# Rows of the destination nodes read from the node table instead of from a second copy by partition, in a four-layer graph network on one core

## The chip, the cores and the metric

One of the cores of a Trainium2 chip runs the whole program; the other cores are idle. The metric is the time of one execution on the device in microseconds, taken several times, with the median given. Beside it stands one execution taken by the hardware profiler, which gives the trace.

## The reference

A network of four graph layers over 50,000 nodes with 64 features and 50,000 edges. The edges are sorted by destination. Before each layer the node features are normalised (layer norm), and what the layer gives is added to them. In short:

```python
h = layernorm(x)
# layer 0: gated convolution, messages summed at dst
z = concat([h[dst], h[src], edge_attr]);  m = sigmoid(z @ W_f + b_f) * softplus(z @ W_s + b_s)
m = m * exp(-distance ** 2 / 9 / 2);      out = segment_sum(m, dst) + h
# layer 1: plain edge network
m = relu(concat([h[src], h[dst], e]) @ W1 + b1) @ W2 + b2;  out = segment_sum(m, dst)
# layer 2: two attention layers of 5 heads (softmax over the edges of a node and a self loop), then a matrix
e = leaky_relu(xl[src] + xr[dst]);        a = softmax over dst of (e . att)
# layer 3: normalised graph convolution W h, batch norm, relu
```

What matters here is that layers 0, 1 and both attention layers need, for each edge, the row `h[src]` (anywhere in the table) and the row `h[dst]`. Since `dst` is sorted, the destinations of 128 neighbouring edges lie close together: some 128 of the 50,000 rows.

## The kernel before, in words

Edges are worked on in 392 tiles (`TILES`) of 128 edges, four tiles to a block (`BLK`), 98 blocks (`NB`) to an edge stage. The program is a sequence of stages; each has its own instruction streams for the five engines and ends when all of them and the DMAs they wait for are done.

1. `setup` (L215 to L552) loads weights and indices and makes lists from them: `lo_i`, for each tile the number of the 128-row block of nodes in which its first destination lies; `rel_d`, for each edge its destination less 128 times that block number; and the list of the tiles whose destinations reach beyond two such blocks.
2. `node_pass(layer)` (L555 to L722) normalises the nodes in 28 groups of 14 tiles of rows (`GRP`), 448 KB each. VectorE writes `h` of a group (L621), in layers 1 and 2 with sums made on ScalarE (L677), in layer 0 with an addition on GpSimd (L656). SyncE then issues, per group, in layer 2 a store of `x` to `x_d` (L715), then `h_d<-h` (L717, the node table, one row of 256 bytes per node), then `near_d<-h` (L718, in layers 0, 1 and 2). `near_d` is a second copy of the table in which row b of partition p is node 128 b + p, so that a partition's own rows lie beside each other and are written in pieces of 3,584 bytes. The ring of `h` buffers comes free when both stores have landed.
3. The edge stages: e0 is `gated_edges` (L931), e1 is `plain_edges` (L1128), l0 and l1 are the two runs of `attention_logits` (L1516). All four use `NearRows` (L791 to L911). GpSimd gathers `h[src]` by an indirect DMA for each tile (`gather`, L870). The rows `h[dst]` are not gathered. `NearRows.load` makes SyncE load, for each tile, the 256 rows of the two blocks that begin at `lo_i[t]` from `near_d` (L882, 64 KB, 512 bytes for each partition), and `relb`, the tile's destinations as offsets, broadcast to all partitions (L877). VectorE compares `relb` with `iota_p`, the number of the row that a partition holds, which gives a one-hot matrix `hotT` (L894). TensorE multiplies it with the rows loaded, onto the transposed `h[src]` (`turn`, L905 and L909). So the destination rows cost a load of neighbouring rows and a matrix product.
4. The far tiles. An edge whose destination lies beyond the window gets its row by a gather: in front of the first block, `fetch_rest`, `mask_rest` and `store_rest` (L823 to L862) run turns of four tiles each (`RING`). In a turn VectorE copies the tile's indices (L838) and a mask (L839), GpSimd gathers the rows of the table (L830), VectorE multiplies them by the mask (L845), and SyncE stores them to `rest_d` (L858); the turn ends when the four stores have landed. `NearRows.load` adds them in again for every block as `z<-rest_d` (L884). `turns` (L813) reads the number of turns from `extra_n`: at least one, else the number of far tiles over four, rounded up. For these inputs 12 tiles reach beyond their two blocks, so each of the four stages runs three turns. The same list tells `extra_pass` (L1392) which sums span more than two blocks.
5. SyncE's order in an edge stage is, for each block, `relb`, a read of four numbers of `lo_i` into registers, the four near loads, `z<-rest_d`, the edge attributes (L976, e0), and the store of the messages of an earlier block (L987, e0). SyncE runs them in that order. Loads are issued up to four blocks (`RINGS`) ahead of TensorE, held back by `z_used`.
6. In l0 and l1 ScalarE's queue loads the destinations of the softmax scan beside that (`acc<-dst_d`, L1486, 15 loads of 200 KB). After l1 the layer goes on as softmax, messages and `attention_nodes` (L1989). With g = 0 the latter writes the table of the second attention layer, `g_d` (L2036), and the copy `near_d<-gout` (L2037, 128 KB, 98 times).

The line that the change touches in every block of every edge stage is L882:

```python
for t in range(BLK):
    sp.dma_start(self.near[k][:, t, :, :], self.S["near_d"][:, ds(los[t], WIN), :]).then_inc(self.near_in[k], 16)
```

Of the kernel before, what the change touches and what calls it, by code (L numbers as in the profile page):

```python
# [21 lines left out]
F32 = mybir.dt.float32  # L22
# [7 lines left out]
P = 128  # L30
# [94 lines left out]
def build(nc, io, out):  # L125
    top = ExitStack()
    with top:
# [6 lines left out]
        h_d = dram("h_d", (TILES * P, C))  # L134
        g_d = dram("g_d", (TILES * P, C))
# [5 lines left out]
        near_d = dram("near_d", (P, TILES + 1, C))  # L141
# [14 lines left out]
        extra_i = sb("extra_i", [1, 3, EXTRA], I32)  # L156
# [58 lines left out]
def setup(nc, io, S):  # L215
# [4 lines left out]
    lo_i, extra_i, extra_n, extra_lo, eps, dst_d = (S[k] for k in ("lo_i", "extra_i", "extra_n", "extra_lo", "eps", "dst_d"))  # L220
    with Phase(nc) as ctx:
# [11 lines left out]
        lo, hi, more, upto, base = (sb(n, [1, TILES]) for n in ("lo", "hi", "more", "upto", "base"))  # L233
        diff_i = sb("diff_i", [1, TILES], I32)
        total_i = sb("total_i", [1, 1], I32)
        col = sb("col", [CT, 2, 4])
        wide_diff = sb("wide_diff", [CT, 4, P])
        step = sb("step", [P, EXTRA])
        passed = sb("passed", [CT, 4, EXTRA])
        a_of = sb("a_of", [P, EXTRA])  # L240
# [5 lines left out]
        turned_col = ctx.enter_context(nc.psum_tensor("turned_col", [P, 2, 4], F32))  # L246
# [90 lines left out]
        with nc.Block() as block:  # L337
            @block.sync
            def _(sp):
# [21 lines left out]
                sp.dma_start(S["near_d"][:, TILES:TILES + 1, :], blank[:, :, 0:C]).then_inc(s_clean, 16)  # L361
# [4 lines left out]
                sp.wait_ge(s_clean, 32)  # L366
# [9 lines left out]
            def _(pool):  # L376
# [7 lines left out]
                nc.gpsimd.iota(S["iota_p"][:, :], pattern=[[P, WIN]], base=0, channel_multiplier=1,  # L384
# [7 lines left out]
            def _(dve):  # L392
# [49 lines left out]
                chain(nc.vector.tensor_tensor_scan(upto[:, :], hi[:, :], more[:, :], 0.0, ALU.mult, ALU.add))  # L442

# [20 lines left out]
                chain(nc.vector.tensor_scalar(a_of[:, :], counted[:, 0, :], float(TILES - 1), None, ALU.min))  # L464
                chain(nc.vector.tensor_copy(extra_i[:, 0, :], a_of[0:1, :]))
                chain(nc.vector.tensor_copy(extra_i[:, 2, 0:1], a_of[0:1, 0:1]))
# [4 lines left out]
                chain(nc.vector.tensor_tensor(extra_i[:, 2, 1:], again[:, 1:], a_of[0:1, 1:], ALU.add))  # L471
# [8 lines left out]
                                                     op0=ALU.mult, op1=ALU.add))  # L480
                dve.sem_inc(s_rel, 1)
# [39 lines left out]
            def _(pe):  # L521
# [12 lines left out]
                nc.tensor.matmul(lo_all[:, :], ones[0:1, :], lo[:, :], start=True, stop=True)  # L534
                pe.wait_ge(s_need, 3)
                for c in range(4):
                    for n, row in enumerate((upto, hi)):
                        mm = nc.tensor.matmul(turned_col[0:CT, n, c:c + 1], row[0:1, c * CT:(c + 1) * CT], ones[0:1, 0:1], start=True, stop=True)
# [3 lines left out]
                pe.wait_ge(s_need, 4)  # L542
# [12 lines left out]
def node_pass(nc, S, layer):  # L555
# [6 lines left out]
    with Phase(nc) as ctx:  # L562
# [23 lines left out]
        def tiles(g):  # L586
            return slice(g * GRP, (g + 1) * GRP)
# [1837 lines left out]
```

## Time and profile before

| what | value |
|---|---|
| median of 3 runs | 6153.05 us (6148.98 to 6160.13) |
| the profiled execution | span 6214.2 us |
| mean granted TensorE clock | 0.845 of full speed |
| busy, of the span: PE, DVE, ACT, POOL | 71%, 53%, 50%, 53% |
| DMA packets, MB | 1,393,493, 665.08 |
| near loads (`near_e`, `near_l`) | 784 + 784 of 64 KB |
| copies `near_d<-h` | 84 of 448 KB |
| copies `near_d<-gout` | 98 of 128 KB |

No time of the profiled execution is listed apart from its span. The span runs from its first instruction to its last and is 61 us, or 1.0%, above the median of the plain runs. The stages lie one behind the other, so a time saved in one of them is saved in the whole, as long as the stage's own limit lies there. The five engines take turns in being the limit: the shares of the whole span say little, and what counts is read stage by stage.

### The profile page before, as it was taken

The page shows a single profiled execution, that of the slowest core. Times are in us where ns is not written, and L with a number is a line of the kernel's source. Part 1 is how long each engine was busy: PE and PEld are TensorE (multiplying, and loading weights), DVE is VectorE, ACT ScalarE, POOL GpSimd, SP SyncE. Part 2 cuts the span into 40 slices and gives each one's busy share as a digit, 9 for nine tenths or more (in the row PEclk, how much of TensorE's full clock was granted, in tenths as well). Part 3 has the DMA queues.
Part 4 walks back from the last instruction along what each step waited for, and adds up shares of the span by engine and source line. Part 5 has one row for each costly group of instructions (what it writes and reads, how often), then busy time and mean ns, then how long its engine had stood idle before and what let it go on. Part 6 is the DMA issues. An engine that isn't in the chain of part 4 may idle for free. (4 is left out here: it accounts for less than half of the span.)

```text
span 6214.2 us, 127051 instructions
## 1 busy us (share of the span) xinstructions
PE 4419.2 (71%) x31655; PEld 3124.8 (50%) x31655; DVE 3312.8 (53%) x7235; ACT 3117.1 (50%) x8158; POOL 3300.7 (53%) x3372
## 2 busy tenths in 40 slices
PE   0078898089896089997498749999669896055564
PEld 0056676066664056665376326666447663054452
DVE  3833333766666432233787963333488788611156
ACT  0267776644555434444386214444358524644447
POOL 0855553155552165553586975555268687666620
PEclk6589998599998599999699979999879998576775
DMA  7545554655554744444133644444323333622224
GB/s 187 169 118 122 123 123 98 176 106 106 109 110 106 241 105 112 113 113 101 33 83 76 153 124 109 113 112 114 83 48 83 77 88 84 138 45 45 44 58 130
DMA packets 1393493, 665.08 MB, mean 107 GB/s; under 512 B 835537, under 2 KB 1341325, under 8 KB 1391594
## 3 DMA queue, kind: packets, MB, share of 16 engines
q1 hardware_dynamic: 1307980, 580.76, 37.4%
q0 software_dynamic: 64256, 65.93, 5.9%
q10 hardware_dynamic: 21124, 17.02, 0.9%
q8 instruction: 35, 0.57, 0.0%
q14 instruction: 98, 0.80, 0.0%
HBM read 393.69 MB, written 269.08 MB: 107 GB/s over the span
## 5 line engine op out<-in xcount | busy, mean ns | idle before, releaser
L870 POOL DMA_INDIRECT z_e<-h_d,src_i x784 | 756.8, 965 | 652.8 <-PE zTp_e L909 453.0
L1656 ACT ACTIVATE leak_l<-tp_l,bcat 128x512 f32<-128x512 f32 x588 | 365.9, 686 | 665.1 <-issue 422.4
L1681 DVE COPY zT_l<-zTp_l 128x512 f32<-128x512 f32 x196 | 135.5, 691 | 1005.7 <-DMA near_d<-gout_a 341.3
L754 ACT ACTIVATE hot_e<-iota_n,rel 128x256 f32<-128x256 f32 x1176 | 501.0, 502 | 322.9 <-DMA hn_a<-g_d 247.2
L784 DVE TENSOR_TENSOR acc<-acc,part_e 128x128 f32 x1176 | 336.8, 286 | 610.1 <-DMA hn_a<-g_d 247.4
L767 PE MATMUL part_e<-z_e,hot_e 128*128 128x128 f32 x1568 | 313.4, 376 | 436.7 <-DVE acc L784 226.9
L870 POOL DMA_INDIRECT z_l<-h_d,src_i x392 | 389.6, 994 | 326.4 <-PE zTp_l L909 229.2
L870 POOL DMA_INDIRECT z_l<-g_d,src_i x392 | 387.9, 989 | 324.9 <-PE zTp_l L909 230.0
L767 PEld LDWEIGHTS part_e<-z_e,hot_e 128*128 128x128 f32 x1568 | 285.2, 279 | 465.0 <-DVE acc L784 240.4
L905 PE MATMUL zTp_e<-ident,z_e 128*128 128x128 f32 x784 | 175.8, 306 | 480.4 <-DMA z_e<-rest_d 472.8
L1351 POOL DMA_INDIRECT z_e<-h_d,src_i x392 | 370.8, 946 | 222.7 <-issue 104.8
L767 PE MATMUL part_e<-m_e,hot_e 128*128 128x128 f32 x3136 | 408.5, 286 | 61.2 <-issue 28.1
L1661 ACT ACTIVATE leak_l<-tp_l,bcat 128x256 f32<-128x256 f32 x784 | 307.8, 475 | 283.1 <-PE tp_l L1618 252.2
L767 PEld LDWEIGHTS part_e<-m_e,hot_e 128*128 128x128 f32 x3136 | 392.5, 200 | 78.4 <-issue 39.9
L767 PEld LDWEIGHTS part_m<-m_m,hot_m 128*128 128x128 f32 x3136 | 365.9, 192 | 88.0 <-DVE acc L784 80.2
L767 PE MATMUL part_m<-m_m,hot_m 128*128 128x128 f32 x3136 | 403.2, 282 | 2.4 <-DVE acc L784 1.1
L1611 PE MATMUL tp_l<-zT_l,wcat 128*128 128x256 f32 x1176 | 376.2, 402 | 22.6 <-DVE zT_l L1681 14.1
L754 ACT ACTIVATE hot_m<-iota_n,rel 128x256 f32<-128x256 f32 x784 | 334.3, 497 | 110.0 <-PE part_m L767 108.5
L905 PEld LDWEIGHTS zTp_e<-ident,z_e 128*128 128x128 f32 x784 | 80.4, 143 | 566.5 <-issue 554.6
L905 PE MATMUL zTp_l<-ident,z_l 128*128 128x128 f32 x784 | 174.1, 304 | 264.8 <-DMA z_l<-rest_d 244.8
L1611 PE MATMUL tp_l<-zT_l,wswap_l 128*128 128x256 f32 x1176 | 355.6, 384 | 1.2 <-issue 1.2
L2179 DVE TENSOR_TENSOR prod_a<-xl_a,wself_a 128x640 f32<-128x640 f32 x392 | 303.9, 815 | 41.7 <-PE xl_a L2073 37.3
(362 smaller groups left out, 11787.7 us busy)
## 6 DMA issues: line engine op xcount, KB each, us to landing
near_e<-near_d SPq DMA_DIRECT2D x784, 64.0 KB
near_l<-near_d SPq DMA_DIRECT2D x784, 64.0 KB
h_d<-h SPq DMA_DIRECT2D x84, 448.0 KB
near_d<-h SPq DMA_DIRECT2D x84, 448.0 KB
m_d<-m_m SPq DMA_DIRECT2D x196, 138.0 KB
relb_e<-rel_d SPq DMA_DIRECT2D x196, 128.0 KB
z_e<-rest_d SPq DMA_DIRECT2D x196, 128.0 KB
relb_l<-rel_d SPq DMA_DIRECT2D x196, 128.0 KB
```

What stands on the lines that cost most here:

```text
L754: ins = self.nc.scalar.activation(self.hots[k][:, t, :], self.S["iota_n"][:, :], ACT.Abs, scale=-1.0, bias=self.S["rel"][:, ds(n * BLK + t ...
L767: mm = self.nc.tensor.matmul(self.parts[t // 2][:, t % 2, w, :], self.hots[k][:, t, w * P:(w + 1) * P], m[:, t, :], start=True, stop=True)
L784: ins = self.nc.vector.tensor_tensor(x, x, part[:, t % 2, :, 0:x.shape[2]], ALU.add)
L870: self.nc.gpsimd.indirect_dma_start(out=self.z[n % RINGS][:, t, SIDES[t % 2]], out_offset=None, in_=self.table[:, :], in_offset=bass.Indir ...
L905: self.nc.tensor.matmul(zTp[:, t * P:(t + 1) * P], self.z[k][:, t, :], ident[:, :], start=(t == 0), stop=False, is_transpose=True, skip_gr ...
L1351: nc.gpsimd.indirect_dma_start(out=z[k][:, t, 0:C], out_offset=None, in_=S["h_d"][:, :], in_offset=bass.IndirectOffsetOnAxis(ap=S["src_i"] ...
L1611: mm = nc.tensor.matmul(by_side(tp[q])[:, side], left[:, q, :], by_side(zT[k])[:, side], start=True, stop=True)
L1656: nc.scalar.activation(leak[u % 2][:, q, :], tp[q][:, :], ACT.Relu, bias=bcat[:, 0, q:q + 1], scale=1.0 - SLOPE).then_inc(leak_ready, 1)
L1661: nc.scalar.activation(by_side(leak[u % 2][:, 3 + q, :])[:, side], tp[3 + side][:, q * 2 * P:(q + 1) * 2 * P].rearrange("p (r e) -> p r e" ...
L1681: nc.vector.tensor_copy(zT[k][:, :], zTp[k][:, :]).then_inc(zT_ready, 1)
L2179: nc.vector.tensor_tensor(prod[k][:, 2 * q:2 * q + 2, :].rearrange("p t (h c) -> p t h c", h=H), xl[slot(u, q)][:, :, 0:HC].rearrange("p t ...
```

## The change

The copy `near_d` is dropped, with all that writes it. The near rows of a tile are loaded from the table itself (`h_d`, or `g_d` in l1), from the tile's first destination on: 256 rows in one piece of 64 KB, of which partition p gets rows 2p and 2p + 1 behind the first. `first_i` holds the first destination of each tile; `ahead` and with it `rel_d` hold each destination less the first one of its tile, and `iota_p` numbers the rows in the new order. Each table gets one more tile of rows, cleared in setup, since a window can reach past the last node. The far tiles of the edge stages get a list of their own, `far_i` with its number of turns in `extra_n[1]`: tiles whose last destination lies 256 or more behind their first. `extra_pass` keeps the old list, and the sums at the destination keep `lo_i` and `rel`. Some buffers move: `digit`, `lof` and `hif` of `plain_edges` into the tail of `acc`, and `din` of `finish` onto `deg_out`.

```diff
-        h_d = dram("h_d", (TILES * P, C))
-        g_d = dram("g_d", (TILES * P, C))
+        h_d = dram("h_d", ((TILES + 1) * P, C))
+        g_d = dram("g_d", ((TILES + 1) * P, C))
-        near_d = dram("near_d", (P, TILES + 1, C))
...
-                sp.dma_start(S["near_d"][:, TILES:TILES + 1, :], blank[:, :, 0:C]).then_inc(s_clean, 16)
+                for table in ("h_d", "g_d"):
+                    sp.dma_start(S[table][TILES * P:(TILES + 1) * P, :].rearrange("(p a) c -> p a c", a=1), blank[:, :, 0:C]).then_inc(s_clean, 16)
...
-                nc.gpsimd.iota(S["iota_p"][:, :], pattern=[[P, WIN]], base=0, channel_multiplier=1,
+                nc.gpsimd.iota(S["iota_p"][:, :], pattern=[[1, WIN]], base=0, channel_multiplier=WIN,
...
+                chain(nc.vector.tensor_copy(first_i[:, :], clipped[0:1, :]))
+                chain(nc.vector.tensor_tensor(wide_one[:, :], ends[:, :], clipped[0:1, :], ALU.subtract))
+                chain(nc.vector.tensor_scalar(wide_one[:, :], wide_one[:, :], float(WIN * P), None, ALU.is_ge))
+                chain(nc.vector.tensor_tensor_scan(far_upto[:, :], hi[:, :], wide_one[:, :], 0.0, ALU.mult, ALU.add))
...
+                chain(nc.vector.tensor_scalar(more[:, 0:1], far_upto[:, TILES - 1:TILES], float(RING - 1), float(RING), ALU.add, ALU.max))
+                chain(nc.vector.tensor_copy(total_i[:, :], more[:, 0:1]))
+                chain(nc.vector.tensor_single_scalar(extra_n[:, 1:2], total_i[:, :], RING.bit_length() - 1, ALU.logical_shift_right))
...
+                    chain(nc.vector.tensor_scalar(far_passed[:, c, :], step[0:CT, :], col[:, 2, c:c + 1], None, ALU.is_ge))
...
+                chain(nc.vector.tensor_tensor(ahead[:, :], dstf[:, :], turned[0][:, :], ALU.subtract))
...
-        outs = 32
+        outs = 32 if layer == 3 else 16
...
-                        sp.dma_start(near_d[:, tiles(g), :], h[k][:, :, :]).then_inc(n_out[two], 16)
...
-        n = eng.value_load(self.S["extra_n"][0:1, 0:1], min_val=1, max_val=EXTRA // RING)
+        n = eng.value_load(self.S["extra_n"][0:1, 1:2], min_val=1, max_val=EXTRA // RING)
...
-        los = self.nc.values_load_multi_w_load_instructions(self.S["lo_i"][0:1, ds(n * BLK, BLK)], engines=(sp.engine,),
+        first = self.nc.values_load_multi_w_load_instructions(self.S["first_i"][0:1, ds(n * BLK, BLK)], engines=(sp.engine,),
...
-            sp.dma_start(self.near[k][:, t, :, :], self.S["near_d"][:, ds(los[t], WIN), :]).then_inc(self.near_in[k], 16)
+            sp.dma_start(self.near[k][:, t, :, :], self.table[ds(first[t], WIN * P), :].rearrange("(p w) c -> p w c", w=WIN)).then_inc(self.near_in[k], 16)
...
-                    sp.dma_start(S["near_d"][:, ds(n * BLK, BLK), :], gout[u % RINGS][:, :, :]).then_inc(g_out[u % RINGS], 16)
```

## Rows read from the trace of the kernel before

**Rows 1.** The page: its first line.

```profile
span 6214.2 us, 127051 instructions
```

**Rows 2.** Windows by stage (e0, node pass 1, e1, node pass 2): start and end, length, busy, clock, DMA.

```profile
319.00:1067.00 748.00, 657.62 (x5488) 509.23 (x5488) 279.90 (x882) 580.15 (x1568) 374.56 (x390) 0.94 0.51 120
...
1089.00:1203.00 114.00, 0.00 (x0) 0.00 (x0) 96.41 (x140) 100.52 (x813) 0.00 (x0) 0.50 0.78 226
...
1240.00:1966.00 726.00, 646.14 (x4901) 458.44 (x4901) 487.55 (x1864) 361.26 (x686) 374.82 (x387) 0.95 0.50 107
...
1990.00:2125.00 135.00, 0.00 (x0) 0.00 (x0) 94.55 (x138) 100.48 (x812) 0.00 (x0) 0.50 0.93 280
```

**Rows 3.** The gathers of far tiles in e0 and e1: count, ns min/median/max.

```profile
L830 POOL DMA_INDIRECT hotT_e<-h_d,left_e x24: 956/962/1126, 292.3 to 1232.5; - x24
```

**Rows 4.** Timeline, far tiles in e0, then e1: start, length, engine, line, work, [idle before].

```profile
299.13 0.25 DVE L845 TENSOR_SCALAR hotT_e<-hotT_e,far_e 128x64 f32<-128x64 f32 x1 [1.13 <-DMA hotT_e<-h_d,left_e]
...
316.99 0.25 DVE L845 TENSOR_SCALAR hotT_e<-hotT_e,far_e 128x64 f32<-128x64 f32 x1 [1.07 <-DMA hotT_e<-h_d,left_e]
...
324.73 0.66 PE L905 MATMUL zTp_e<-ident,z_e 128*128 128x128 f32 x2 [281.11 <-DMA z_e<-rest_d]
...
1217.21 0.25 DVE L845 TENSOR_SCALAR hotT_e<-hotT_e,far_e 128x64 f32<-128x64 f32 x1 [0.92 <-DMA hotT_e<-h_d,left_e]
...
1235.02 0.26 DVE L845 TENSOR_SCALAR hotT_e<-hotT_e,far_e 128x64 f32<-128x64 f32 x1 [0.98 <-DMA hotT_e<-h_d,left_e]
```

**Rows 5.** Timeline, far tiles in l0, then in l1.

```profile
2128.14 7.10 ACTq L1486 DMA_DIRECT2D acc<-dst_d  x15
...
2152.69 0.19 POOL L829 TENSOR_TENSOR spare_l<-iota_p 128x1 f32<-128x1 f32 x1 [1.16 <-DMA rest_d<-hotT_l]
...
2169.60 0.35 SPq L877 DMA_DIRECT2D relb_l<-rel_d  x1
...
3684.77 0.20 POOL L829 TENSOR_TENSOR spare_l<-iota_p 128x1 f32<-128x1 f32 x1 [1.10 <-DMA rest_d<-hotT_l]
...
3701.55 0.35 SPq L877 DMA_DIRECT2D relb_l<-rel_d  x1
```

**Rows 6.** Timeline, node pass 1: its first h, its last issues, the next stage.

```profile
1100.97 1.09 DVE L621 SCALAR_TENSOR_TENSOR h<-xc,rstd 128x896 f32<-128x896 f32 x1
...
1195.45 1.18 SPq L717 DMA_DIRECT2D h_d<-h  x1
1196.68 2.08 SPq L718 DMA_DIRECT2D near_d<-h  x1
1203.59 0.39 DVE L1280 MEMSET deg_in<- 128x393 f32 x1 [8.16 <-PEq L87]
```

**Rows 7.** Timeline, node pass 2: its first h, two groups' issues of h_d, the next stage.

```profile
1997.90 1.09 DVE L621 SCALAR_TENSOR_TENSOR h<-xc,rstd 128x896 f32<-128x896 f32 x1
...
2006.10 1.22 SPq L717 DMA_DIRECT2D h_d<-h  x1
...
2010.71 1.23 SPq L717 DMA_DIRECT2D h_d<-h  x1
...
2128.21 0.09 DVE L1691 MEMSET alate_l<- 128x32 f32 x1 [17.87 <-PEq L87]
```

**Rows 8.** Timeline of setup: the wait on VectorE.

```profile
127.89 0.21 DVE L485 CAST cut_b<-b 3x128 bf16<-3x128 f32 x1 [85.48 <-DMA bn<-in_L_gnn_beta_dram]
```

**Rows 9.** L882, the issues of the near loads: ns min/median/max.

```profile
L882 SPq DMA_DIRECT2D near_e<-near_d x784: 2/333/1047, 320.3 to 1941.0; - x196
```

**Rows 10.** Timeline, SyncE in e0: near loads of two blocks.

```profile
503.98 4.46 SPq L882 DMA_DIRECT2D near_e<-near_d  x4
...
511.99 2.18 SPq L882 DMA_DIRECT2D near_e<-near_d  x4
```

**Rows 11.** TensorE's wait for the near loads in e1 (us, times, longest).

```profile
PE zTp_e L905 <- DMA z_e<-rest_d: 191.7, 28, 154.4
```

**Rows 12.** What VectorE waited for at L894 (us, times).

```profile
  DMA relb_e<-rel_d: 208.9, 84
```

More of the change, by code:

```diff
@@ L155, in build @@
         lo_i = sb("lo_i", [1, TILES], I32)
-        extra_i = sb("extra_i", [1, 3, EXTRA], I32)
+        first_i = sb("first_i", [1, TILES], I32)
+        ahead = sb("ahead", [P, TILES])
+        far_i = sb("far_i", [1, 2, EXTRA], I32)
+        extra_i = sb("extra_i", [1, 2, EXTRA], I32)
         extra_n = sb("extra_n", [1, 4], I32)
@@ L220, in setup @@
     lo_i, extra_i, extra_n, extra_lo, eps, dst_d = (S[k] for k in ("lo_i", "extra_i", "extra_n", "extra_lo", "eps", "dst_d"))
+    first_i, ahead, far_i = (S[k] for k in ("first_i", "ahead", "far_i"))
     with Phase(nc) as ctx:
@@ L534, in _ @@
                 nc.tensor.matmul(lo_all[:, :], ones[0:1, :], lo[:, :], start=True, stop=True)
+                nc.tensor.matmul(turned[0][:, :], ones[0:1, :], clipped[0:1, :], start=True, stop=True)
                 pe.wait_ge(s_need, 3)
                 for c in range(4):
-                    for n, row in enumerate((upto, hi)):
+                    for n, row in enumerate((upto, hi, far_upto)):
                         mm = nc.tensor.matmul(turned_col[0:CT, n, c:c + 1], row[0:1, c * CT:(c + 1) * CT], ones[0:1, 0:1], start=True, stop=True)
@@ L542, in _ @@
                 pe.wait_ge(s_need, 4)
+                for c in range(4):
+                    nc.tensor.matmul(turned[1][:, 0:EXTRA], ones[0:CT, :], far_passed[:, c, :], start=(c == 0), stop=(c == 3))
                 for n, left in enumerate((None, wide_diff)):
@@ L550, in _ @@
                 for c in range(4):
-                    tr = nc.tensor.transpose(rel_rows[:, c, :], rel[:, c * CT:(c + 1) * CT], ident[:, :])
+                    tr = nc.tensor.transpose(rel_rows[:, c, :], ahead[:, c * CT:(c + 1) * CT], ident[:, :])
                 tr.then_inc(s_ends, 1)
 def node_pass(nc, S, layer):
-    acc3, h_d, x_d, near_d, eps, deg_out = (S[k] for k in ("acc3", "h_d", "x_d", "near_d", "eps", "deg_out"))
+    acc3, x_d, eps, deg_out = (S[k] for k in ("acc3", "x_d", "eps", "deg_out"))
+    h_d = S["h_d"][0:TILES * P, :]
     G, DEEP = TILES // GRP, 4
@@ L819, in tiles @@
     def tiles(self, eng, i, row, most):
-        return self.nc.values_load_multi_w_load_instructions(self.S["extra_i"][0:1, row, ds(i * RING - RING, RING)], engines=(eng.engine,),
+        return self.nc.values_load_multi_w_load_instructions(self.S["far_i"][0:1, row, ds(i * RING - RING, RING)], engines=(eng.engine,),
                                                              min_val=0, max_val=most,
@@ L854, in body @@
         def body(i):
-            a = self.tiles(sp, i, 2, TILES + EXTRA - 1)
+            a = self.tiles(sp, i, 1, TILES + EXTRA - 1)
             for k in range(RING):
@@ L877, in load @@
         sp.dma_start(self.relb[k][:, :], self.S["rel_d"][ds(n * BLK * P, BLK * P)].rearrange("(a e) -> a e", a=1).broadcast_to([P, BLK * P])).then_inc(self.relb_in[k], 16)
-        los = self.nc.values_load_multi_w_load_instructions(self.S["lo_i"][0:1, ds(n * BLK, BLK)], engines=(sp.engine,),
-                                                            min_val=0, max_val=TILES - 1,
-                                                             skip_runtime_bounds_check_because="setup clamps the node of an edge to N - 1 ahead of taking its tile")[1]
+        first = self.nc.values_load_multi_w_load_instructions(self.S["first_i"][0:1, ds(n * BLK, BLK)], engines=(sp.engine,),
+                                                              min_val=0, max_val=N - 1,
+                                                              skip_runtime_bounds_check_because="setup clamps the node of an edge to N - 1")[1]
         for t in range(BLK):
-            sp.dma_start(self.near[k][:, t, :, :], self.S["near_d"][:, ds(los[t], WIN), :]).then_inc(self.near_in[k], 16)
+            sp.dma_start(self.near[k][:, t, :, :], self.table[ds(first[t], WIN * P), :].rearrange("(p w) c -> p w c", w=WIN)).then_inc(self.near_in[k], 16)
         sp.dma_start(self.z[k][:, :, :].rearrange("p (r t) c -> p r (t c)", t=2)[:, :, C:3 * C],
@@ L2052, in _ @@
                     for k in range(RINGS):
[L2053 removed]
+                        sp.wait_ge(g_out[k], 16 * len(range(k, NB, RINGS)))
             @block.tensor
```

33 lines of the change are left out of this document (18 added, 15 removed).

## The prediction

> **What bounds the kernel now.** I read the windows by stage first, then the timeline at the seams of the stages, then the waits of the lines that the change touches. The stages follow one another, so the whole is a sum of stages, each with its own limit. In e0 and e1 TensorE is busy for 657.6 of 748 us and 646.1 of 726 us, with the DMA engines at half load [rows 2]: TensorE is the limit, with some 90 and 80 us in which it waits. In node pass 1 ScalarE works 100.5 of 114 us with the DMA engines at 0.78. Node pass 2 has the same 100.5 us of ScalarE, but takes 135 us, at a DMA share of 0.93 [rows 2]: there the stores are the limit. Between a node pass and the first matrix product of the edge stage lie the turns of far tiles, in which every engine waits for a gather, a product, a store and the next gather [rows 4].
>
> The sum is made in times of the profiled execution, whose span of 6214.2 us [rows 1] stands 61 us above the median of the runs. The savings are waits on transfers and issues, so I take them off the median as they are; scaled by the 1.0% between the two they would change by 1 us. A measurement of this kernel can tell about 0.2%, 12 us, from no change.
>
> **The far tiles.** The inputs decide how many turns run. Before, 12 tiles reach over the end of their two blocks of nodes, since a window that starts at a block's edge wastes what lies ahead of the first destination. The trace has 24 gathers in e0 and e1 together [rows 3], which is 12 a stage, or three turns. Worked out from the destinations, the largest distance within a tile from its first edge to its last is 169 rows, below 256. So no tile is far after the change, and the minimum of one turn is left: two turns go in each of the four stages.
>
> In e0 the last mask of turn 1 is at 299.13 and that of turn 3 at 316.99, so two turns take 17.86 us; in e1 it is 1235.02 less 1217.21, 17.81 us [rows 4]. All that follows (the store's landing, `relb`, the near loads, the first product at 324.73) hangs on the last turn, because SyncE waits for its stores ahead of the first load of a block. Nothing else is late there: GpSimd's gathers of `h[src]` need only room in their ring. I take the whole 35.7 us. From below it can't be less than a few us under that, since the remaining turn keeps its own length.
>
> In l0 and l1 the same two turns take longer, because ScalarE's queue moves 15 loads of 200 KB at that time [rows 5]. After the change these loads still run when SyncE gets to its first block. What the rows show is when the stores of turn 1 landed: GpSimd's wait for the last of them ended at 2152.69 in l0, and SyncE's first `relb` stood at 2169.60; in l1 it is 3684.77 and 3701.55 [rows 5]. That is 16.9 and 16.8 us by which `relb` can move up. The first near loads then meet the end of that traffic. In turn 1 and 2 a transfer took a few us more than in turn 3; I take 3 us of the gain away for it, which leaves 14 us each, 28 together. The bounds are 10 (near loads as slow as the stores of turn 1) and 26 (all the two turns), for each.
>
> **The copies.** Node pass 2 loses 28 copies of 448 KB. Then it has per group one store in rows of 256 bytes and one in pieces of 3,584 bytes, which is just what node pass 1 has before, and the same ScalarE work. From its first `h` to the next stage node pass 1 takes 1203.59 less 1100.97, 102.6 us [rows 6], and node pass 2 takes 2128.21 less 1997.90, 130.3 us [rows 7]. The difference is 27.7 us, and I take it. It fits the distance of two groups' `h_d` stores, 4.61 us [rows 7], against ScalarE's 100.5/28 = 3.59 us: 27 x 1.02 = 27.5 us. What is late next is ScalarE. Bounds 24 and 30.
>
> Node pass 1 loses its copies too, but its limit is ScalarE. Only the end moves. The copy's issue takes 2.08 us behind that of `h_d`, and the next stage follows 4.83 us behind its end [rows 6]; with the same distance behind `h_d` the gain is 2.1 us, bounds 0 and 4. Node pass 0 is held by GpSimd's additions; for its end I take 1 us, bounds 0 and the 2.1 of node pass 1. The 98 copies of `attention_nodes` lie beside other work, and the last one at its end is a 128 KB store: 0.5 us, bounds 0 and 1. If their cover went, it would be VectorE's work that is gone, and nothing takes it away.
>
> **What is added.** Setup gets some fifteen small instructions on VectorE, a scan among them, and a few products. They stand ahead of a wait of 85.48 us for a weight load [rows 8], which covers them; without that cover they would cost some 5 us by like instructions. Two blank stores take the place of one. SyncE's queue in an edge stage keeps its instructions: `relb`, four register reads, four loads, `rest`. The near loads have the same 64 KB and the same 128 pieces of 512 bytes; only their distance in memory changes, from 100,608 bytes to 512. No row of this trace has both forms, so I bound it. Four near loads hold SyncE for 4.46 us in one block and 2.18 us in the next [rows 10], with a median of 333 ns for one [rows 9]. I take no change, the middle between these two, as bytes, count and piece stay, and give the ends to the rivals.
>
> Here the Trainium skill has a rule, under "DMA: Bandwidth & Descriptors", section "Latency and other measured facts": copies between memory tensors lose up to half their rate when the 128 partitions read at a pitch of some MiB that is a power of two, and laying a tile out contiguously is one of the two cures. By it the new form is safe and the old one, with a pitch that is no power of two, was not slow either, so that the sum would stay. The page calls the cause, channels shared by streams in lock step, an inference. Were one piece of 64 KB to fall on few channels, that cause would speak against the change; no run here shows it yet.
>
> **The sum.** 35.7 + 28 + 27.7 + 2.1 + 1 + 0.5 = 95.0 us. 6153.05 less 95 is 6058 us, 1.5% less.
>
> **The rivals.**
>
> A. Contiguous loads free SyncE. In e0 SyncE is behind: VectorE waited 208.9 us for `relb` in 84 blocks [rows 12], and in e1 TensorE waited 191.7 us for the near loads, 154.4 of it at the start, so 37.3 us within the stage [rows 11]. If four loads always took 2.18 us, e0 could close up to TensorE's 657.6 us, 90 us less, and e1 win the 37: 6058 less 127 is 5931 us. Half of it would be 5995. For it speaks that reads of one piece are the simplest there are; against it that the stalls look like those of the issue, whatever is loaded. By the rule quoted above it would not happen, as the old pitch was harmless.
>
> B. They hold SyncE longer. The place is the same, L882 in e0 and e1. If every block took 4.46 us in place of an even mix of both, that is 1.14 us for each of 196 blocks, 223 us if all of it shows: 6281 us, slower than before. It decides from 95/196 = 0.48 us per block, that is 0.12 us per near load on a median of 0.33 [rows 9]. Gathers and near loads now read one table, and its windows start at any row. Against it: the DMA engines are at half load [rows 2], and l0 and l1 have no wait of this kind to speak of.
>
> C. The traffic in l0 and l1 is no hindrance. Then the two turns give up to 26 us each, 24 us more than I take: 6034 us.
>
> D. The list does not get short: some tile counts as far and there are three turns still, or the padded slots do. Then 35.7 + 28 us are not won: 6122 us. The destinations speak against it, with 169 below 256.
>
> **How the numbers follow.** My forecast, at 6058 give or take 15, has 0.58; C 0.14; A, mostly in part, 0.18; D 0.03; B 0.07, of which one hundredth or two stops near no change. The range takes in the forecast with its bounds on the high side (the smallest terms sum to 31 + 20 + 24 = 75 us, 6078, and a fifth of B's price on top is just above 6100), C, and half of A: 5998 to 6098. Faster by over 0.2% is all of the forecast, C, A and D but a hundredth or two, 0.92; same 0.02; slower 0.06.
>
> **What would show it.** In the profile after: 16 gathers of far tiles on L830 in the four stages, in place of 48; e0's first product some 18 us nearer to the end of node pass 0; in l0 the first `relb` some 24 us behind the stage's start in place of 41; node pass 2 at some 103 us from its first `h`, with ScalarE's groups 3.6 us apart and a DMA share near 0.8; windows of e0 and e1 at 748 and 726 us as before. The forecast is wrong if these two windows differ by over 10 us, or if node pass 2 stays above 110 us.

## The result and the profile after

The changed kernel takes 6039.18 us (median of 4 runs, 6036.0 to 6047.74), beside 6154.98 us for the kernel before in the same comparison: a ratio of 0.9815, 95% interval 0.9803 to 0.9827. That is 116 us less; the prediction had 95 us less and 6058 us, with a range from 5998 to 6098.

One thing must be known before any two traces are set side by side. The kernel before, the very same program, took 6155 us here, but 6217 us in one later series and 5836 us in three, each of these four on a chip of its own, with a spread of at most 0.4% within each. The first profile of the kernel before has a span of 6214 us where its runs took 6155, and the one of the kernel after a span of 6037 us where its runs took 6039. The two don't come from like conditions. What follows takes from these two only what does not depend on that (node passes and the seams, the stretches from an edge stage's start to its first matrix product), and compares the long loops within one series.

The page of the kernel after, span and granted clock, which answers to [rows 1]:

```profile
span 6036.7 us, 126285 instructions
...
PEclk6599998599997699997898989999699897567775
```

The same four windows as [rows 2]: e0, node pass 1, e1, node pass 2.

```profile
299.00:1018.00 719.00, 647.08 (x5488) 499.91 (x5488) 280.15 (x880) 580.10 (x1568) 367.69 (x383) 0.97 0.54 124
1040.00:1150.00 110.00, 0.00 (x0) 0.00 (x0) 96.26 (x140) 100.51 (x813) 0.00 (x0) 0.50 0.59 118
1164.00:1878.00 714.00, 638.70 (x4901) 453.42 (x4901) 487.41 (x1866) 361.01 (x686) 379.20 (x392) 0.95 0.52 109
1901.00:2011.00 110.00, 0.00 (x0) 0.00 (x0) 96.15 (x140) 99.14 (x812) 0.00 (x0) 0.50 0.88 234
```

Node pass 2 fell from 135 to 110 us at nearly the same ScalarE work (100.5 and 99.1 us), and its DMA rate from 280 to 234 GB/s. Node pass 1 has the same 110 us. The loops e0 and e1 are 29 and 12 us shorter by these windows, with the same products and the same loads; no trace of the kernel before is from the conditions of this result, so these two numbers are not the change's, see below.

The timeline of node pass 2 after, which answers to [rows 7]: the first `h`, two groups' stores of `h_d`, the last stores, the next stage.

```profile
1910.47 1.09 DVE L641 SCALAR_TENSOR_TENSOR h<-xc,rstd 128x896 f32<-128x896 f32 x1
...
1915.13 0.38 SPq L737 DMA_DIRECT2D h_d<-h  x1
...
1918.67 0.38 SPq L737 DMA_DIRECT2D h_d<-h  x1
...
2003.62 0.38 SPq L737 DMA_DIRECT2D h_d<-h  x1
...
2004.96 1.18 SPq L737 DMA_DIRECT2D h_d<-h  x1
...
2011.85 0.09 DVE L1711 MEMSET alate_l<- 128x32 f32 x1 [6.92 <-PEq L87]
```

Two stores of `h_d` are 3.54 us apart, as ScalarE's work sets it, where it was 4.61. From the first `h` to the next stage it is 101.4 us, where it was 130.3: 28.9 us less. Node pass 1, which answers to [rows 6], went from 102.6 to 99.9 us:

```profile
1051.01 1.09 DVE L641 SCALAR_TENSOR_TENSOR h<-xc,rstd 128x896 f32<-128x896 f32 x1
...
1150.90 0.39 DVE L1300 MEMSET deg_in<- 128x393 f32 x1 [5.07 <-PEq L87]
```

The turn of far tiles in e0, which answers to [rows 4]: the first copy of indices, the first and the last mask, SyncE's first `relb`, the first product.

```profile
281.24 0.10 DVE L857 COPY left_e<-dst_i 128x1 int32 x1
...
286.11 0.26 DVE L864 TENSOR_SCALAR hotT_e<-hotT_e,far_e 128x64 f32<-128x64 f32 x1 [4.26 <-DMA hotT_e<-h_d,left_e]
...
291.39 0.25 DVE L864 TENSOR_SCALAR hotT_e<-hotT_e,far_e 128x64 f32<-128x64 f32 x1 [1.27 <-DMA hotT_e<-h_d,left_e]
...
293.70 0.18 SPq L896 DMA_DIRECT2D relb_e<-rel_d  x1
...
299.51 0.66 PE L924 MATMUL zTp_e<-ident,z_e 128*128 128x128 f32 x2 [247.57 <-DMA z_e<-rest_d]
```

One turn is left. The first product follows 8.1 us behind the last mask (it was 7.7), but the one turn takes longer than each of the three did: 10.2 us from its first copy to its last mask, where turn 1 of the kernel before took 8.0 (291.16 to 299.13; turns 2 and 3 took 7.7 each). Its first copy in the profile before:

```profile
291.16 0.10 DVE L838 COPY left_e<-dst_i 128x1 int32 x1
```

The 8 gathers in e0 and e1 together are one turn in each, so rival D is out. VectorE waited 16.9 us in 8 masks for them:

```profile
L849 POOL DMA_INDIRECT hotT_e<-h_d,left_e x8: 957/961/1126, 282.4 to 1162.1; - x8
...
  DVE hotT_e L864: 16.9, 8
```

In l0, which answers to [rows 5], the rows are the node loads, the last mask, the first `relb`, the first product:

```profile
2011.78 6.70 ACTq L1506 DMA_DIRECT2D acc<-dst_d  x15
...
2025.82 0.25 DVE L864 TENSOR_SCALAR hotT_l<-hotT_l,far_l 128x64 f32<-128x64 f32 x1 [1.51 <-DMA hotT_l<-h_d,left_l]
...
2037.85 0.35 SPq L896 DMA_DIRECT2D relb_l<-rel_d  x1
...
2046.89 0.66 PE L924 MATMUL zTp_l<-ident,z_l 128*128 128x128 f32 x2 [147.68 <-DMA z_l<-rest_d]
```

The last mask stands at 2025.82, and SyncE can start only 12.0 us later, when the last store has landed. The first product comes 35.1 us behind the node loads' first issue, where it was 47.1 us (2175.21 less 2128.14).

Within e1, TensorE's wait for its loads, which answers to [rows 11], is 168.7 us with 136.9 at the start, so 31.8 us within the stage, where it was 37.3:

```profile
PE zTp_e L924 <- DMA z_e<-rest_d: 168.7, 28, 136.9
```

Setup ended earlier too. The wait which covers the new instructions, [rows 8], ended at 120.83 in place of 127.89:

```profile
120.83 0.22 DVE L501 CAST cut_b<-b 3x128 bf16<-3x128 f32 x1 [70.10 <-DMA bn<-in_L_gnn_beta_dram]
```

### The profile page after: what moved, and what is told of

Its sections match the earlier page's. It is cut to its first block and busy times, and to the rows that moved or that the text cites. A ratio compares the mean times of both kernels' runs of the same rounds, so it can differ in the third digit from the quotient of the medians.

```text
span 6036.7 us, 126285 instructions
## 1 busy us (share of the span) xinstructions
PE 4385.9 (73%) x31673; PEld 3103.9 (51%) x31673; DVE 3297.6 (55%) x7153; ACT 3114.5 (52%) x8158; POOL 3264.2 (54%) x3308
## 5 line engine op out<-in xcount | busy, mean ns | idle before, releaser
L1975 DVE TENSOR_TENSOR prod_m<-xl_m,al 128x640 f32<-128x640 f32 x392 | 305.1, 820 | 35.4 <-issue 18.2
```

The lines of the kernel that those rows point to most:

```text
L1975: nc.vector.tensor_tensor(heads[:, 2 * q:2 * q + 2], xl[slot(u, q)][:, :, 0:HC].rearrange("p t (h c) -> p t h c", h=H), wide(al[:, ds(n * ...
```

## The experiments

Each was timed in the same series as the kernel before, on one chip. There are four series, on four chips: one where the kernel before takes 6217.8 us (experiments 1 to 4), and three where it takes 5836.9 (5 to 7), 5836.1 (the repeats and 10) and 5836.4 (11). "From the start to the first product" is, by the trace, from a stage's first instruction to TensorE's first product in it.

### 1. The kernel before, once more

No edit.

> The kernel before, unchanged, for a second profile. The first profile has a span 61 us above the median of the plain runs, the one of the changed kernel only 2 us less than its run. If the first profile was a long one, this one comes out near 6155 us, and its edge stages e0 and e1, setup and the last stages are shorter than 779, 762 and 147 us by some 61 us in all. If the profiler itself costs 1% on this kernel, it comes out near 6214 us again.

Measured: 6216.9 us (11 runs) beside 6217.8; ratio 0.9997, interval 0.9988 to 1.0006. Its profile has a span of 6222.6 us, 6 us from the median of its own runs. So the profiler costs next to nothing, and the first profile is that of an execution under conditions in which the kernel takes 6215 us, not 6155. The 6214 us of the second expectation came again, but not for its reason. The page's first line, and SyncE's register instructions at L877:

```profile
span 6222.6 us, 127051 instructions
...
L877 SPq FUSED_REGOPS  x360: 2/60/728, 357.8 to 4422.0; - x180
```

Where the kernel before takes 6217 us, a SyncE instruction that has a median of 60 ns now and then takes 0.7 us. The trace of the kernel after, from the chip of the timed result, has the same (L901, the near loads):

```profile
L901 SPq FUSED_REGOPS  x1568: 2/37/726, 294.3 to 4244.7; - x196
...
L901 SPq DMA_DIRECT2D near_e<-h_d x784: 2/333/718, 294.4 to 1853.9; - x196
```

and the trace of the same kernel where the kernel before takes 5836 us has none among the register instructions:

```profile
L901 SPq FUSED_REGOPS  x1568: 37/37/47, 296.5 to 4026.0; - x196
...
L901 SPq DMA_DIRECT2D near_e<-h_d x784: 332/333/1359, 296.6 to 1655.9; - x196
```

By the trace, the changed kernel's e0 has 228 SyncE instructions of 0.64 to 0.8 us in the first and 1 in the second. From its first product on it takes 719 us in the first, and 616 us in the second.

### 2. One turn, all else as before

It leaves out the rows of the far tiles of turns 2 and 3.

```diff
                 chain(nc.vector.tensor_single_scalar(extra_n[:, 0:1], total_i[:, :], RING.bit_length() - 1, ALU.logical_shift_right))
+                chain(nc.vector.memset(extra_n[:, 1:2], 1))
...
-        n = eng.value_load(self.S["extra_n"][0:1, 0:1], min_val=1, max_val=EXTRA // RING)
+        n = eng.value_load(self.S["extra_n"][0:1, 1:2], min_val=1, max_val=EXTRA // RING)
```

> The kernel before, with one turn of far tiles in each edge stage in place of three; it leaves out the rows of the far tiles of turns 2 and 3. Theory 1 (the sum of the prediction, two turns are worth 18 us in e0 and e1 and 14 us in l0 and l1): 64 us less than before, 6091 us. Theory 2 (what was won above the sum lies in l0 and l1, whose turns give their whole 26 us): 88 us less, 6067 us.

Measured: 6135.7 us, 82 us less, ratio 0.9866 (0.9851 to 0.9881), between the two theories. The trace tells more: from the start to the first product e0 fell from 36.1 to 17.7 us, e1 from 39.2 to 21.2, l0 from 47.5 to 35.3, l1 from 46.5 to 35.5. That is 18.4, 18.0, 12.2 and 11.0, 59.6 us in all. Theory 2 is false: l0 and l1 give less than 14, not 26. The other 22 us lie where nothing was edited. Between the two profiled executions it is 88.6 us, and the 29 us beyond the seams lie in the loops behind the first product: 5.3 us in e0, 2.8 in e1, 8.1 in l0 and 12.6 in l1.

### 3. Three turns in the changed kernel

```diff
-                chain(nc.vector.tensor_single_scalar(extra_n[:, 1:2], total_i[:, :], RING.bit_length() - 1, ALU.logical_shift_right))
+                chain(nc.vector.memset(extra_n[:, 1:2], 3))
```

> The changed kernel, with three turns forced in each edge stage. The mirror of the run before: theory 1 expects 64 us more than the changed kernel's 6039 us, 6103 us; theory 2 expects 88 us more, 6127 us.

Measured: 6194.6 us, ratio 0.9963 (0.9951 to 0.9975); the changed kernel itself was not in that series, so the difference to it is not measured. What counts is the seam: from the start to the first product e0 takes 45.0 us and e1 48.0, where the kernel before, with three turns as well, takes 36.1 and 39.2. Each turn of the changed kernel is 3 us longer there than one of the kernel before. In l0 (54.1 against 47.5 us) and l1 (52.1 against 46.5) it is some 2 us.

### 4. The copies written again, read by nothing

```diff
+        near_d = dram("near_d", (P, TILES + 1, C))
...
-        outs = 32 if layer == 3 else 16
+        outs, near_d = 32, S["near_d"]
...
+                        sp.dma_start(near_d[:, tiles(g), :], h[k][:, :, :]).then_inc(n_out[two], 16)
...
+                    sp.dma_start(S["near_d"][:, ds(n * BLK, BLK), :], gout[u % RINGS][:, :, :]).then_inc(g_out[u % RINGS], 16)
```

> The changed kernel, with the copies by partition written again in node passes 0 to 2 and in attention_nodes, and read by nothing. Theory 1: 31 us more than the changed kernel, 6070 us, 28 of them in node pass 2. Together with the kernel before at one turn it tells the form of the near loads apart, since both write the copies and run one turn: if the form is worth nothing the two are equal; if the 20 us above the sum are the form's, this one is 20 us faster.

Measured: 6145.1 us, ratio 0.9877 (0.9862 to 0.9893). Against the one-turn kernel of the same series (6135.7) it is 9 us more, with intervals that overlap. What the copies cost can't be read here, since the changed kernel was not in that series; experiments 8 and 9 tell it. The seams are longer in e0 (22.3 against 17.7 us), e1 (25.8 against 21.2) and l1 (38.2 against 35.5).

### 5. The changed kernel, on a quicker chip

> The changed kernel, unchanged, beside the kernel before on one chip. The kernel before took 6217 us in the last series and 6155 us in the first, so times of different series are not to be set side by side; this run gives the changed kernel's stages beside the next ones. By the ratio measured it comes out at 0.9815 of the kernel before, 6103 us where that takes 6217. If the difference between series lies in the stages that the change touches, the ratio will differ as well.

Measured: 5742.4 us beside 5836.9; ratio 0.9841 (0.9827 to 0.9854), 94.5 us less. A last such run in the third series:

> The changed kernel once more, so that the whole way from the kernel before to it is seen on one chip together with the next two runs. The ratio should lie between the two measured, 0.9815 and 0.9841.

Measured: 5744.0 us beside 5836.1; ratio 0.9842 (0.9829 to 0.9856), 92 us less. Where SyncE's long instructions are absent, the gain is what the sum of the prediction had, 95 us. The ratio did not lie between the two expected, as it is the second again.

### 6. No turn at all

It leaves out the far tiles' rows, of which these inputs have none.

```diff
-                near.fetch_rest(pool)
...
-                near.mask_rest(dve)
...
-                near.store_rest(sp)
```

> The changed kernel with no turn of far tiles at all: it leaves out the rows of far tiles, of which there are none here. It prices the one turn that is left. Theory 1 (what SyncE can start on is held by the stores of the turn): 11 us less in e0 and e1 each, and 15 to 20 us in l0 and l1 each, as SyncE's first load then stands right at the stage's start: some 55 us less than the changed kernel. Theory 2 (in l0 and l1 the traffic of the 15 loads holds the first block whatever comes before it): some 10 us each in l0 and l1, 40 us less in all.

Measured: 5708.6 us beside the changed kernel's 5742.4, 34 us less. From the start to the first product e0 fell from 19.9 to 8.0 us and e1 from 23.6 to 8.0, l0 only from 35.5 to 34.2 and l1 from 36.3 to 33.3. Theory 2 holds, and more strictly than it said. The rows of l0 are the node loads and the first product:

```profile
1801.67 2.12 ACTq L1500 DMA_DIRECT2D acc<-dst_d  x4
...
1835.83 0.66 PE L924 MATMUL zTp_l<-ident,z_l 128*128 128x128 f32 x2 [147.16 <-DMA z_l<-rest_d]
```

SyncE's first `relb` is at 1804.80 here, and still TensorE waits until 1835.83: the first blocks come late, whatever stands in front. That it is the 15 loads of 200 KB which hold them is shown by the next experiment, which moves these loads away.

### 7. The node loads behind the first block

```diff
+                act.wait_ge(near.near_in[0], 80)
                 scans.load_nodes(act, S["dst_d"])
...
-                        scans.masks(dve, chain, n)
+                        for step in {3: (1,), 4: (2, 3), 5: (4, 5)}.get(n, ()):
+                            scans.masks(dve, chain, step)
```

> The changed kernel, in which ScalarE issues the 15 loads of 200 KB in l0 and l1 only when the first block's loads have landed, with VectorE's use of them two blocks later. If the traffic is what holds the one turn (in l0 its last mask stands at 2025.82 in the profile after, and SyncE's first load only 12 us later), the first product comes 12 to 15 us earlier in l0 and in l1, and the kernel is 20 to 30 us faster than the changed one. If the turn is slow for another reason, nothing is won, and VectorE's wait for the loads costs a few us.

Measured: 5777.9 us, 35 us more than the changed kernel. In l0 the first rows come as expected, and then the loop stalls. The rows are the stage's start, the node loads, the first product, SyncE's near loads of block 3, the first product of block 1:

```profile
1826.04 0.57 SPq L1589 DMA_DIRECT2D wswap_l<-wcat  x1
...
1844.96 6.36 ACTq L1506 DMA_DIRECT2D acc<-dst_d  x15
...
1845.18 0.66 PE L924 MATMUL zTp_l<-ident,z_l 128*128 128x128 f32 x2 [131.72 <-DMA z_l<-rest_d]
...
1856.76 10.97 SPq L901 DMA_DIRECT2D near_l<-h_d  x4
...
1861.29 0.66 PE L924 MATMUL zTp_l<-ident,z_l 128*128 128x128 f32 x2 [12.72 <-issue]
```

The first product is 19.1 us behind the start, where it was 35.5. But four near loads then take SyncE 10.97 us, and TensorE stands still for 12.7 us ahead of block 1. From the first product to the end l0 takes 758.6 us in place of 724.7, l1 763.0 in place of 726.4. Moving the loads into the running loop costs twice what it saves. Not all of it is traffic, though: compared block by block with the changed kernel, l0 is 24.9 us behind when block 3 begins and l1 28.2, all of it before VectorE starts on these loads. The other 9 us of each are lost by the start of block 7, while VectorE does its work on them (20.8 us), which the edit moved as well; what of this is traffic was not told apart.

### 8 and 9. The way from one kernel to the other, step by step

The one-turn kernel and the one with copies again, now beside the changed kernel in one series.

> The kernel before with one turn of far tiles, again, now beside the changed kernel. Where the kernel before took 6217 us, this was 82 us less (ratio 0.9866), more than the prediction's 64 us. If turns always give that, the ratio is 0.987 here too; on a chip where the kernel before takes some 5837 us the prediction's 64 us would be a ratio of 0.989.

> The changed kernel with the copies by partition written but not read, again, beside the changed kernel. The step from the one-turn kernel to this one is the form of the near loads: 9 us more in the first series (6145 against 6136 us), which would speak for a small loss; the prediction had none. If it is noise of that series, the two are equal within 5 us here. The step from this one to the changed kernel is the copies: the prediction has 31 us.

| kernel | median, us | ratio to before (interval) | step, us |
|---|---|---|---|
| before | 5836.1 | | |
| one turn | 5770.3 | 0.9884 (0.9869 to 0.9899) | -65.9 |
| + loads from the table, own list | 5779.3 | 0.9903 (0.9888 to 0.9919) | +9.0 |
| + no copies = the changed kernel | 5744.0 | 0.9842 (0.9829 to 0.9856) | -35.2 |

The prediction had 64, 0 and 31 for the three. The step of 9 us is the same in both series, though the intervals of the two ratios overlap in each. By the trace it is no matter of the loops: from the first product on, e0 takes 616.7 us with one turn and the loads by partition, 614.6 with those from the table, e1 619.2 and 618.8, l0 726.9 and 724.9, l1 725.6 and 727.0. It is in the seams again: 17.3 to 20.1, 21.2 to 23.1, 33.1 to 37.2, 32.9 to 37.9 us, 13.8 in all. Setup gives some of it back, 146.6 to 141.1 us.

Node pass 2 in the one-turn kernel of this series takes 141.6 us, at a DMA share of 0.90 and with the same 100.5 us of ScalarE; in the changed kernel 111.1:

```profile
1720.80:1862.40 141.60, 0.00 (x0) 0.00 (x0) 96.32 (x140) 100.47 (x812) 0.00 (x0) 0.50 0.90 273
```

### 10. The first near loads ahead of the turn's stores

```diff
+        for n in range(2):
+            self.load_near(sp, n, n)
...
+        if has(n, 2):
+            self.load_near(sp, n, u)
...
+                dve.wait_ge(self.rest_out[k], 16 * i + 16)
```

> The changed kernel, in which SyncE issues relb and the near loads of blocks 0 and 1 ahead of the stores of the one turn that is left, and not behind their landing; VectorE then waits for these stores itself before it writes hotT. Theory 1 (between the stores' landing and the first product lie SyncE's issues and the near loads, 5.8 us in e0): 3 us less in each stage, and up to 5 in l0 and l1, some 15 us in all. Theory 2 (the loads only take the place of others, as with the late node loads): no gain, within 5 us.

Measured: 5742.4 us beside 5744.0: nothing. The seams of e0 and e1 are 1.9 and 2.7 us shorter, those of l0 and l1 2.3 and 4.5 longer. In l0 the stores of the turn, which now stand behind the early loads, hold SyncE for 12.1 us, where it was 6.7. Theory 2 for l0 and l1, theory 1 for e0 and e1, and the sum is zero (setup came out 2.6 us shorter in this trace, with no edit there).

### 11. Empty slots that point to tile 0

```diff
                 chain(nc.vector.tensor_scalar(a_of[:, :], turned[1][:, 0:EXTRA], float(TILES - 1), None, ALU.min))
+                chain(nc.vector.scalar_tensor_tensor(out=a_of[:, :], in0=a_of[:, :], scalar=float(TILES - 1), in1=a_of[:, :],
+                                                     op0=ALU.is_lt, op1=ALU.mult))
```

> The changed kernel, in which the empty slots of a turn point to tile 0 in place of tile 391, by one more instruction in setup. Tile 391 holds only padding, so that its 128 indices all name row 49,999 and each of the four gathers reads one row 128 times; tile 0 has about as many different rows as edges. Theory 1 (the gathers and stores of a turn are slow because all read one row: from the stage's start to the first product e0 takes 19.9 us against 17.3 in the one-turn kernel of the old list, e1 23.3 against 21.2, l0 36.1 against 33.1, l1 37.4 against 32.9): these four come back, 8 to 12 us less than the changed kernel, 5733 us where that takes 5743, with e0 at 17.3 from the start to the first product. Theory 2 (the longer turn comes from the table being read by the near loads as well): nothing changes, within 3 us.

Measured: 5731.2 us beside 5836.4; ratio 0.9823 (0.981 to 0.9837), 105 us less than before, 13 us less than the changed kernel's 5744.0 in the series before. The changed kernel was not in this series; the kernel before takes the same time in both, but the intervals of the two ratios (0.9829 to 0.9856 for the changed kernel) overlap, so that the 13 us are uncertain and what counts is the traces. The gathers of e0 and e1 in three kernels: instruction, VectorE's waits for them, and the time from issue to landing. With one turn of the old list, whose slots are real tiles:

```profile
L831 POOL DMA_INDIRECT hotT_e<-h_d,left_e x8: 954/958/1122, 291.9 to 1069.2; - x8
...
  DVE hotT_e L846: 12.4, 8
...
DMA to landing us min/median/max: 2.3/2.4/2.6
```

The changed kernel:

```profile
L849 POOL DMA_INDIRECT hotT_e<-h_d,left_e x8: 952/958/1123, 284.6 to 1061.4; - x8
...
  DVE hotT_e L864: 16.8, 8
...
DMA to landing us min/median/max: 3.5/3.9/4.7
```

With the empty slots on tile 0:

```profile
L851 POOL DMA_INDIRECT hotT_e<-h_d,left_e x8: 952/958/1125, 284.5 to 1056.8; - x8
...
  DVE hotT_e L866: 12.4, 8
...
DMA to landing us min/median/max: 2.3/2.4/2.6
```

By the inputs, the 128 indices of tile 0 name 83 different rows, those of the 12 far tiles of the old list 76 to 94, and those of tile 391 one. A gather of such a tile of real edges lands in 2.4 us, one of the same row 128 times in 3.9 us, at the same 0.96 us of GpSimd. VectorE's waits go from 12.4 to 16.8 and back to 12.4 us. From the start to the first product e0 takes 17.5 us (changed kernel 19.9), e1 21.2 (23.3), l0 34.6 (36.1), l1 36.0 (37.4). That is 7.4 us in all, of the 8 to 12 expected. Theory 1 holds for e0 and e1, which are back at the one-turn kernel's values (17.3 and 21.2) within 0.2 us, so that the table being read by two kinds of load has no part there. In l0 and l1 it holds for a half and a third of the difference; what makes up the rest, 1.5 and 3.1 us, stays open.

## Why the prediction was right, and where its terms were off

**The bound, read stage by stage.** It held. Node pass 2 was bound by its stores, and without the copies ScalarE is its limit; the seams and the ends of the stages gave the rest.

**Two turns in e0 and e1, 35.7 us.** Right for turns as they were: 18.4 and 18.0 us in the one-turn kernel. What failed is the clause "the remaining turn keeps its own length". With no far tile left, all four slots of the turn point to the last tile, which is padding and names one row 128 times. The seams are 2.6 and 2.1 us longer (19.9 against 17.3, 23.3 against 21.2), and pointing the slots elsewhere takes 2.4 and 2.1 of it back. The prediction knew that the slots would be padded, and asked only whether that made a far tile, not what the gather would cost.

**Two turns in l0 and l1, 28 us.** The mechanism was right, the traffic of the node loads, and rival C, by which that traffic is no hindrance, is false. The size was off. Two turns less gave 12.2 and 11.0 us, not 14 each, and no turn at all gives 1 to 3 more. The 3 us that the prediction took off for the end of the traffic should have been 5 to 6; in the first profiles the whole seam went from 47.1 to 35.1 us in l0 and from 47.0 to 37.3 in l1.

**Node pass 2, 27.7 us.** 28.9 us in the first profiles, 30.5 in the third series (141.6 to 111.1 us). The pattern chosen, node pass 1 of the kernel before, still had its own copy at its end, 2.8 us of it; it was taken off for node pass 1 and not for node pass 2. With it the term is 30.5, just above the upper bound of 30.

**Node passes 1 and 0, 2.1 and 1 us.** 2.8 us each (113.9 to 111.1 and 141.1 to 138.3). GpSimd's additions do not hide the last copy of node pass 0, as the 1 us taken for it had it. `attention_nodes` gave 0.3 to 0.4 us for 0.5, which is no more than the spread between traces of kernels alike in that stage.

**What is added, 0.** The new instructions are hidden as said, though the prediction's "some 5 us by like instructions" was low: the wait that hides them begins at 50.7 us in place of 42.4 in the first profiles, 8.3 us later. Yet the wait that hides them ended 4 to 7 us earlier, at 120.83 in place of 127.89 in the first profiles and at 123.05 in place of 127.33 in the third series. It is there with copies and without, so it came with the setup of the new form; two blank stores of 128 rows in one piece each stand there now in place of one in rows 100,608 bytes apart. Which of setup's edits does it was not tried.

**The form of the near loads, 0.** Right. One near load has a median of 333 ns at SyncE before and after. Rival B is false by the quicker series: from the first product on the four stages differ by 2.1 us at most between the two forms. Rival A can't be judged there, since nothing is left to win: TensorE is busy for 607.9 of the 616.7 us of e0's loop in the one-turn kernel, and VectorE's wait for `relb` is 6.7 us. It can be judged in the slow series, where SyncE is behind. The rows are e0's loop in the one-turn kernel, then in the one with loads from the table and copies, both where the kernel before takes 6217 us, then the first of them where that takes 5836:

```profile
305.80:1049.60 743.80, 660.57 (x5488) 512.90 (x5488) 278.61 (x880) 581.85 (x1568) 371.07 (x385) 0.94 0.52 120
...
305.50:1049.90 744.40, 659.15 (x5488) 510.98 (x5488) 279.68 (x880) 579.85 (x1568) 364.80 (x382) 0.95 0.51 120
...
305.80:922.50 616.70, 607.93 (x5488) 481.48 (x5488) 277.25 (x880) 580.29 (x1568) 378.20 (x385) 0.99 0.63 145
```

VectorE waits 155.5 us for `relb` in the first and 166.6 us in the second, so the form frees nothing of SyncE's time: rival A is false too. The room that A saw was real, some 127 us in e0, but it goes with SyncE's 0.7 us instructions, which both forms have in the slow series and neither (but for one or two) in the quick one. So 64 KB in one piece or in 128 pieces at a pitch of 100,608 bytes, from a table that is gathered from at the same time or from one that isn't, takes the stages the same time. The rule of the Trainium skill weighed there ("DMA: Bandwidth & Descriptors", "Latency and other measured facts") is not put to the test by this. The page has its loss at pitches of 2 MiB and more, and by the page a 4 MiB pitch padded by 192 bytes, which is no power of two, was slow as well; so the prediction's reason, that a pitch which is no power of two is harmless, is more than the page says. This case shows no loss at 100,608 bytes (616.7 against 614.6 us in e0) and no sign of the inferred cause, shared channels, on one piece of 64 KB.

**The sum.** In the quicker series it came out at 92 to 95 us for the 95 forecast, with errors that nearly cancel, which is luck: 12 us lost in the turn that is left (2.6, 2.1, 3.0 and 4.5 in the four seams, of which 7.4 came back with the padded slots) and 5 too many in l0 and l1, against 5 won in the node passes and 4 in setup; a few us stay without a place. In the first comparison it was 116 us, and two turns less gave 82 in the slowest series where 60 lie in the seams. There the traces place most of the rest: the loops of l0 and l1 take 1516.6 us together in the kernel before and 1511.8 us in the changed kernel with three turns, but 1495.9 and 1496.3 us in the two kernels with one turn. Those of e0 and e1 show no such order (1473.1 and 1459.1 us against 1465.0 and 1470.7). No edit touches these loops. Why those of l0 and l1 are 16 to 21 us shorter behind a shorter seam, and what SyncE's 0.7 us instructions wait for, stays open. It is known for that series alone: of the first comparison, whose 21 us above the sum look alike, there is no trace of the kernel before.

Two slips in the range did no harm. Half of rival A, 5995 us, lies outside the 5998 to 6098 that was to take it in, and a fifth of B's price on top of 6078 is 6123 us, not just above 6100.

**The forecast of the loops.** The prediction said it would be wrong if the windows of e0 and e1 differed by over 10 us, and by its first two profiles they do, by 29 and 12. Two executions under different conditions were compared there. Within one series the loops of the two forms, from the first product on, differ by at most 9.4 us in e0 and 5.1 in e1 (slow series, three turns, then one), and by 2.1 and 0.4 in the quick one. The other signs came near: e0's first product 15.3 us nearer to the stage's start for 18, l0's first `relb` at 26.1 us for 24, node pass 2 at 101.4 us for 103, at a DMA share of 0.88 for 0.8.

Of the versions that do all the work the last one has the lowest ratio, 0.9823, and seams 7.4 us shorter than the changed kernel's.

## What to carry to other kernels

When a change empties a list, price what the loop does with an empty one: the least number of turns runs on padding, and padding that names one address everywhere can be slower than real work. Point it at ordinary data. For a pass that is bound by stores, look for one in the same kernel with the load that the changed one will have, and take off from it, too, what the change takes off from both. And before two traces are set side by side, see whether the kernel that did not change has the same stage lengths in both.

## What the runs showed of the hardware that was not expected

- An indirect gather of 128 rows of 256 bytes from issue to landing: 2.4 us for a tile of real edges, with some 80 different rows (2.3 to 2.6), 3.9 us for one row 128 times (3.5 to 4.7), 8 each.
- The same program took 6155.0, 6217.8, 5836.9, 5836.1 and 5836.4 us in five series, the last four on four different chips, each with a spread below 0.4%. The traces of the slower two have some 230 to 270 SyncE instructions of 0.64 to 0.8 us in e0 and in e1 each, the quicker ones none to two; the changed kernel's node passes 1 and 2 take the same 111.1 us in both. For one and the same program, the one-turn kernel, the 6135.7 and 5770.3 us differ in few stages: from the first product on e0 takes 743.8 and 616.7 us, e1 721.2 and 619.2, l0 and l1 some 22 more each, and the edge stage of layer 3 598.5 and 510.6. Whether the chip makes the difference or something else of the series was not told apart. The change's ratio was 0.9815 in one series, 0.9841 and 0.9842 in others.
- 3 MB of loads that start with a stage hold its first product until 33 to 38 us, with one turn of far tiles in front of it or with none. When they started only 19 us later, beside the first blocks, in l0 and l1, the loops took 34 and 37 us more, of which 25 and 28 were lost in blocks 0 to 2.
